# Routed tiles halved in row layout, shared blocks stored plainly and routed results added by scatter, in a kernel with a scan layer and a mixture of experts

## Chip, cores and metric

One NeuronCore of a Trainium2 chip runs one program. The metric is the device time of one execution in microseconds. Six queues of instructions run side by side: TensorE (PE, its weight loads PEld), VectorE (DVE), ScalarE (ACT), GpSimd (POOL), SyncE (SP, here it only issues DMAs). Each works in program order; semaphores order them against each other.

## Reference

The input is 16 sequences of 512 tokens with 128 features. Two layers, each with a normalisation before it and a residual after it:

```python
x = x + state_space(layernorm(x))       # h_t = a*h_(t-1) + B x_t ;  y = C h + D x
x = x + moe(layernorm(x))

# moe, x of 8192 tokens:
shared = (silu(x @ wg.T) * (x @ wu.T)) @ wd.T          # every token
top_id, score = argmax(logits), sigmoid(max(logits))   # logits = x @ gate_w.T, 8 experts
for e in range(8):                                     # the token's one expert
    xe = where(top_id == e, x * score, 0)
    routed += (silu(xe @ wg[e].T) * (xe @ wu[e].T)) @ wd[e].T
return shared + routed
```

The hidden width is 256. So every output row is x1 (the row after the first layer) + shared + routed.

## The kernel before

**First part.** The sequences run in 8 pairs: normalise, transpose, B product, scan along the 512 tokens, C product, residual into `x1`, second normalisation into `n2`, transposed copies `n2T_hi` and `n2T_lo` (fp16, a number as the sum of two halves; `w_split` holds the weights of gate and up likewise, so that a product is three fp16 products). The array `rows` holds for each token x1, n2, its number and its top logit in 264 numbers (1,056 bytes). In groups of 16 token tiles (a tile is 128 tokens) `route` picks the expert of each token and `places` gives it a row in `table`, a DRAM array in which the tokens of an expert lie together. `scatter_row` (L1043) has GpSimd write the 128 whole rows of a token tile to these places by one indirect DMA, 64 in all.

**Shared blocks.** A block is 512 tokens, 16 in all. `shared_gate_up` makes 12 products, ScalarE the silu (`shared_silu`), VectorE the product (`shared_hidden`), `shared_down` 16 fp32 products. The order of blocks is written out: blocks 8 to 15 first (EARLY), then 0 to 7 (LATE). For the first eight VectorE adds the result to x1 in `rows` (`base`, L867), and the rows of these tokens are scattered after that, with x1 + shared in them. The rows of tokens of blocks 0 to 7 are scattered before with x1 alone, and ScalarE copies their shared result over x1 in SBUF (`late_base`, L589). Five of the late blocks (MIDDLE) run before the routed tiles, three behind them. Between the blocks stand parts of other work, by fixed block numbers (`if b == 5:` and so on): the last route, the fp16 halves of routed weights, and the map (`map_counts` to `map_rows`) that says which rows of the table and which expert each routed tile has. SP waits for the map's last step (MAP), the pads that fill up the table, and all scattered rows, then loads the tiles (L277).

**Routed tiles.** There are 39: 32 of 256 rows and 7 of 128, in a ring of 12 buffers. For each: ScalarE computes two tiles' scores from the top logits (`tile_score`) and scales n2 by the score in place (`tile_scale`); TensorE transposes it in fp32 into a PSUM bank (`transpose_tile`); ScalarE copies to fp16 (`tile_hi`), VectorE makes the low half from bank and copy (`tile_lo`); then `routed_gate_up` (12 products), `routed_silu`, `routed_hidden`, `routed_down` (8), and `routed_result`, which adds the tile's x1 part and writes it into the ring buffer. GpSimd scatters 128 rows of 512 bytes to `out` per instruction (`scatter_result`, L1082), two for a whole tile, 71 in all. When all have landed, it adds the eight late blocks of shared results to `out` by accumulating DMAs (`add_late`, L1090).

The order in each queue in the routed stage, for tile j:

```python
PE:  routed_gate_up(j)  routed_down(j - 1)  transpose_tile(j + 2)
ACT: routed_silu(j)  [tile_score(j + 4), j even]  tile_hi(j + 2)  tile_scale(j + 4)
DVE: routed_hidden(j)  routed_result(j - 1)  tile_lo(j + 2)
```

Of the kernel before, what the change touches and what calls it, by code (L numbers as in the profile page):

```python
# [17 lines left out]
ROW = 264  # L18
PITCH = 66
# [9 lines left out]
LATE = 8  # L29
MIDDLE = 5  # L30
# [22 lines left out]
def block_kernel(nc, x, weights, consts, tri_ones, token_ids, pads, out):  # L53
# [12 lines left out]
    EARLY = BLOCKS - LATE  # L66
    FIRST = EARLY + MIDDLE
# [16 lines left out]

    table = nc.dram_tensor("table", (E * REGION + E * SLOTS, ROW), F32, kind="Internal").ap()

    with ExitStack() as ctx:
# [3 lines left out]
        def sem(name):  # L91
# [81 lines left out]
        x_rings = (w_line[:, 0:IN_WEIGHTS * SH * ROW].rearrange("p (k s r) -> p k s r", k=IN_WEIGHTS, s=SH),  # L173
                   sb("x_ring", [P, XRING - IN_WEIGHTS, SH, ROW])[:])
        x_in = [x_rings[k // IN_WEIGHTS][:, k % IN_WEIGHTS] for k in range(XRING)]
        xT_hi = [sb(f"xT_hi{k}", [P, SLOTS], F16) for k in range(XTRING)]
        xT_lo = [sb(f"xT_lo{k}", [P, SLOTS], F16) for k in range(XTRING)]
# [51 lines left out]
        s_first_rows = [sem(f"late_rows_scattered{k}") for k in range(4)]  # L229
# [3 lines left out]
        s_late = sem("sh_late_ready")  # L233
        s_out = sem("output_stored")
        s_xin = [sem(f"tile_loaded{k}") for k in range(XRING)]
        s_xt, s_xh, s_xl = sem("tile_transposed"), sem("tile_hi"), sem("tile_lo")
# [5 lines left out]

        def block_of(b):
            return (b + LATE) % BLOCKS

# [6 lines left out]
        def _(sp):  # L252
# [41 lines left out]
            for k in range(4):  # L294
                sp.wait_ge(s_first_rows[k], 16 * LATE * BT // 4)
                sp.wait_ge(s_scattered[k], 16 * EARLY * BT // 4)
            for j in range(TILES):
                load_tile(j)
            sp.wait_ge(s_out, 16 * LATE)

        @block.tensor
        def _(pe):
# [79 lines left out]
            def shared_gate_up(b):  # L382
                tok = slice(block_of(b) * SEQ, (block_of(b) + 1) * SEQ)
                pe.wait_ge(s_lo, block_of(b) + 1)
# [46 lines left out]
            def routed_gate_up(j):  # L431
# [4 lines left out]
                for kind, banks, used, done in ((0, gate_bank, r_silu, r_g), (1, up_bank, r_hid, r_u)):  # L436
                    after(pe, used, j - 1)
                    for c in range(FC):
                        o = banks[j % 2][:, w * c:w * (c + 1)]
                        mm(o, w_of(kind, e, 0, c), xT_hi[k][:, 0:w], start=True, stop=False)  # L440
                        mm(o, w_of(kind, e, 0, c), xT_lo[k][:, 0:w], start=False, stop=False)  # L441
                        last = mm(o, w_of(kind, e, 1, c), xT_hi[k][:, 0:w], start=False, stop=True)  # L442
# [36 lines left out]
            for b in range(FIRST):  # L479
# [49 lines left out]

        @block.scalar  # L530
        def _(act):
# [57 lines left out]
            def late_base(b):  # L589
                n = block_of(b)  # L590
                act.wait_ge(s_o, b + 1)
                if b == EARLY:
                    for k in range(4):
                        act.wait_ge(s_first_rows[k], 16 * LATE * BT // 4)
                run(x1[:, n * BT:(n + 1) * BT, :], down_bank[b % 2][:].rearrange("p (t d) -> p t d", t=BT),
                    ACT.Copy).then_inc(s_late, 1)
# [31 lines left out]
            def tile_score(j):  # L628
# [7 lines left out]
                run(tanh[:, of, 0:n], tops[:, :, 0:n, 2 * D + 1], ACT.Tanh, scale=l_scale[:, 0:1]).then_inc(s_tanh, 1)  # L636
# [3 lines left out]
            def tile_scale(j):  # L640
                k = j % XRING
                act.wait_ge(s_score, j // 2 + 1)
                for s in range(halves(j)):
                    last = run(x_in[k][:, s, D:2 * D], x_in[k][:, s, D:2 * D], ACT.Copy, scale=score[:, k, s:s + 1])
                last.then_inc(s_scaled, 1)

            def tile_hi(j):
# [3 lines left out]
                run(xT_hi[j % XTRING][:, 0:w], tile_bank[j % 2][:, 0:w], ACT.Copy).then_inc(s_xh, 1)  # L651
# [507 lines left out]
```

## Time and profile before

| | |
|---|---|
| Time, median of 3 runs | 280.43 us (279.65 to 280.5) |
| Profiled execution | 279.88 us, span of its instructions 277.6 us |
| Mean granted TensorE clock | 0.957 |
| Busy: PE, DVE, ACT, POOL | 84%, 65%, 62%, 53% of the span |
| Moved by DMA | 37.83 MB, mean 136 GB/s |

The span runs from the first to the last instruction; the execution takes 2.3 us more. The first part lasts to about 95 us, the shared blocks to about 150 us, the routed tiles to about 255 us, then the late blocks are added. In the rows below, times are microseconds from the start of the span. "idle before" is the time in which the engine stood still ahead of the instructions, and the arrow names what ended it. A row of a timeline with x2 or x8 merges instructions that followed each other. Where a line of the kernel gives way to a number as L87 or L1152, that is a helper or the runtime's own barrier.

### The profile page before, as it was taken

Reading aid. Unit: us, or ns where it says so; the run is one execution under the profiler, and the core shown is the slowest. Engines: PE = TensorE matmul, PEld = TensorE weight load, DVE = VectorE, ACT = ScalarE, POOL = GpSimd, SP = SyncE. Lnnn points to the kernel's source line nnn. Section 1 sums busy time; section 2 is a strip of 40 time slices with the busy share of each in tenths; the row PEclk is TensorE's granted clock in tenths of the full one; section 3 lists DMA queues with packets and bytes.
Section 4 is the critical chain, followed back from the end, with each engine's and each line's share of the span. In section 5 each row is a group of like instructions: output and inputs, shape, how many; then the busy total and the mean of one; then the engine's idle time right before and its main releaser. Section 6 shows DMA issues by size and latency. Waiting matters only on the chain. (4 is left out here: it accounts for less than half of the span.)

```text
span 277.6 us, 6124 instructions
## 1 busy us (share of the span) xinstructions
PE 233.6 (84%) x1891; PEld 181.1 (65%) x1891; DVE 179.9 (65%) x512; ACT 173.0 (62%) x415; POOL 146.2 (53%) x150
## 2 busy tenths in 40 slices
PE   0584988878779999999997699999999999999900
PEld 0263655565367466676774599999999999765700
DVE  3599998799887986559873156666666666644200
ACT  2753988996997984643342686777767676723400
POOL 1000000017777777778770027777777777775940
PEclk9999597999999999999999799999999999999975
DMA  6999500002323223232853923655465543211991
GB/s 210 396 333 327 218 0 0 2 1 101 116 100 119 100 106 110 100 117 97 284 206 105 297 99 93 167 170 172 132 176 165 143 121 96 72 47 50 107 175 22
DMA packets 24862, 37.83 MB, mean 136 GB/s; under 512 B 3680, under 2 KB 16864, under 8 KB 24272
## 3 DMA queue, kind: packets, MB, share of 16 engines
q1 hardware_dynamic: 15264, 22.03, 26.0%
q0 software_dynamic: 9568, 15.41, 19.9%
q8 instruction: 17, 0.28, 0.5%
q14 instruction: 13, 0.11, 0.1%
HBM read 22.03 MB, written 19.73 MB: 150 GB/s over the span
## 5 line engine op out<-in xcount | busy, mean ns | idle before, releaser
L1045 POOL DMA_INDIRECT table<-rows,place x64 | 65.6, 1024 | 60.2 <-DVE place L808 41.1
L1086 POOL DMA_INDIRECT out<-w_full x51 | 49.5, 970 | 33.5 <-DVE w_full L1022 19.5
L1015 DVE SCALAR_TENSOR_TENSOR hid<-bank,h_scale,n1T 128x512 f32<-128x512 f32 (+1 forms) x39 | 27.4, 703 | 29.8 <-ACT n1T L657 28.4
L440 PE MATMUL bank<-xT_hi,w_split 128*128 128x256 f16 (+1 forms) x156 | 40.9, 264 | 0.8 <-DVE xT_lo L1007 0.5
L442 PE MATMUL bank<-xT_hi,w_split 128*128 128x256 f16 (+1 forms) x156 | 40.9, 264 | 0.0
L441 PE MATMUL bank<-xT_lo,w_split 128*128 128x256 f16 (+1 forms) x156 | 40.7, 263 | 0.0
L452 PE MATMUL bank<-w_full,hid 128*128 x284 | 38.7, 277 | 0.1
L587 ACT ACTIVATE n1T<-bank,g_scale 128x512 f32<-128x512 f32 x32 | 21.8, 687 | 23.3 <-PE bank L394 23.1
L452 PEld LDWEIGHTS bank<-w_full,hid 128*128 128x128 f32 x284 | 34.8, 192 | 1.4 <-issue 0.2
L406 PEld LDWEIGHTS bank<-w_full,hid 128*128 128x128 f32 x256 | 32.4, 200 | 1.8
L406 PE MATMUL bank<-w_full,hid 128*128 128x128 f32 x256 | 32.6, 283 | 0.0
L563 ACT ACTIVATE rows<-rows,nb,r 128x128 f32<-128x128 f32 x64 | 25.6, 481 | 6.9 <-DVE nb L764 6.9
L651 ACT ACTIVATE xT_hi<-bank 128x256 f16<-128x256 f32 (+1 forms) x39 | 14.2, 364 | 24.3 <-PE bank L413 24.3
L864 DVE SCALAR_TENSOR_TENSOR hid<-bank,h_scale,n1T 128x512 f32<-128x512 f32 x32 | 23.3, 748 | 9.3 <-ACT n1T L587 8.6
L657 ACT ACTIVATE n1T<-bank,g_scale 128x512 f32<-128x512 f32 (+1 forms) x39 | 25.0, 640 | 2.6 <-PE bank L442 2.4
L549 ACT ACTIVATE n<-rows,nb,r 128x128 f32<-128x128 f32 x64 | 25.4, 480 | 1.0 <-DVE nb L727 1.0
L310 PE MATMUL bank<-const,n 128*128 128x128 f32 x64 | 12.2, 328 | 15.3 <-ACT n L549 15.3
L392 PE MATMUL bank<-n2T_hi,w_split 128*128 128x512 f16 x64 | 24.3, 380 | 0.8 <-DVE w_full L1022 0.4
L394 PE MATMUL bank<-n2T_hi,w_split 128*128 128x512 f16 x64 | 24.3, 379 | 0.0
L393 PE MATMUL bank<-n2T_lo,w_split 128*128 128x512 f16 x64 | 24.2, 379 | 0.0
L1007 DVE TENSOR_TENSOR xT_lo<-bank,xT_hi 128x256 f16<-128x256 f32 (+1 forms) x39 | 15.6, 401 | 13.2 <-PE bank L406 8.9
L1086 POOL DMA_INDIRECT out<-x_ring x20 | 19.4, 970 | 6.1 <-issue 5.5
(142 smaller groups left out, 432.6 us busy)
## 6 DMA issues: line engine op xcount, KB each, us to landing
w_full<-table SPq DMA_DIRECT2D x24, 264.0 KB, 3.0
rows<-in_x SPq DMA_DIRECT2D x8, 512.0 KB, 7.8
w_full<-in_weights SPq DMA_DIRECT2D x3, 1152.0 KB, 12.7
table<-in_pads SPq DMA_DIRECT2D x1, 2112.0 KB, 10.5
table<-in_pads SPq DMA_DIRECT2D x8, 264.0 KB, 4.2
x_ring<-table SPq DMA_DIRECT2D x8, 264.0 KB, 3.3
out<-rows POOLq DMA_DIRECT2D x8, 256.0 KB, 7.8
table<-rows,place POOLq DMA_INDIRECT x64, 2.4
```

The source lines that it names most:

```text
L392: mm(o, w_split[:, 0, kind, 0, f], n2T_hi[:, tok], start=True, stop=False)
L406: last = mm(o, hid[2 * par + c][:, tok], w_full[:, 2, f], start=(c == 0), stop=(c == FC - 1))
L440: mm(o, w_of(kind, e, 0, c), xT_hi[k][:, 0:w], start=True, stop=False)
L441: mm(o, w_of(kind, e, 0, c), xT_lo[k][:, 0:w], start=False, stop=False)
L442: last = mm(o, w_of(kind, e, 1, c), xT_hi[k][:, 0:w], start=False, stop=True)
L452: last = mm(o, hid[j % 4][:, slot], down_of(j, c), start=(c == 0), stop=(c == FC - 1))
L549: last = run(n1[:, t, :], x1[:, q * PT + t, :], ACT.Identity, bias=nb1[q % 2][:, t:t + 1], scale=r1[q % 2][:, t:t + 1])
L563: last = run(n2[:, i, :], x1[:, i, :], ACT.Identity, bias=nb2[q % 2][:, t:t + 1], scale=r2[q % 2][:, t:t + 1])
L657: run(silu[j % 2][:, 0:w], gate_bank[j % 2][:, 0:w], ACT.Silu, scale=g_scale[:, 0:1]).then_inc(r_silu, 1)
L1015: v.scalar_tensor_tensor(out=hid[j % 4][:, 0:w], in0=up_bank[j % 2][:, 0:w], scalar=h_scale[:, 0:1], in1=silu[j % 2][:, 0:w], op0=ALU.mult ...
L1045: g.indirect_dma_start(table[:, :], bass.IndirectOffsetOnAxis(ap=place[:, i:i + 1], axis=0), rows[:, i, :], None).then_inc(done, 16)
L1086: g.indirect_dma_start(out[:, :], bass.IndirectOffsetOnAxis(ap=x_in[k][:, s, 2 * D:2 * D + 1].bitcast(I32), axis=0), x_in[k][:, s, 0:D], N ...
```

## The change

- `table` keeps only n2, number and top logit: 136 numbers a row, 544 bytes. `rows` stays as it is; the scatter takes its last 136 numbers.
- The blocks run in the order 0 to 15, all before the routed tiles. VectorE adds each result to x1 (`base`), and SP stores the block to `out` with a plain DMA (`store_block`), in fixed places of its order: blocks 0 to 8 ahead of the pads, 9 to 11 behind them, 12 to 15 behind the loads of the first four tiles. The rows are scattered without a wait for `base`.
- A tile is split before it is transposed: ScalarE writes the scaled high half in fp16 (`tile_scale`), VectorE the low half from the loaded tile, the score and the high half (`tile_low`), TensorE turns both by products with an fp16 identity, and ScalarE copies both at once from PSUM (`tile_copy`).
- `routed_result` is a copy. The scatter to `out` adds (`compute_op=ALU.add`), and GpSimd waits for all 16 stores before the first one. `late_base` and `add_late` are gone.

```diff
+TILE_ROW = 136
-LATE = 8
-MIDDLE = 5
...
-    table = nc.dram_tensor("table", (E * REGION + E * SLOTS, ROW), F32, kind="Internal").ap()
+    table = nc.dram_tensor("table", (E * REGION + E * SLOTS, TILE_ROW), F32, kind="Internal").ap()
...
+        identity_h = sb("identity_h", [P, P], F16)
+        x_half = [sb(f"x_half{k}", [P, 2, SH, P], F16) for k in range(XTRING)]
+        xT = [sb(f"xT{k}", [P, 2, SLOTS], F16) for k in range(XTRING)]
...
+            def store_block(b):
+                sp.wait_ge(s_base, b + 1)
+                sp.dma_start(out_tiles[:, b * BT:(b + 1) * BT, :], x1[:, b * BT:(b + 1) * BT, :]).then_inc(s_out, 16)
+
+            for b in range(9):
+                store_block(b)
             sp.wait_ge(s_map, 1)
             for e in range(E):
                 store_pads(e)
+            for b in range(9, 12):
+                store_block(b)
...
             for k in range(4):
-                sp.wait_ge(s_first_rows[k], 16 * LATE * BT // 4)
-                sp.wait_ge(s_scattered[k], 16 * EARLY * BT // 4)
-            for j in range(TILES):
+                sp.wait_ge(s_scattered[k], 16 * NT // 4)
+            for j in range(4):
                 load_tile(j)
-            sp.wait_ge(s_out, 16 * LATE)
+            for b in range(12, BLOCKS):
+                store_block(b)
+            for j in range(4, TILES):
+                load_tile(j)
+            sp.wait_ge(s_out, 16 * BLOCKS)
...
-                after(pe, s_base, min(b - 1, EARLY))
-                after(pe, s_late, b - 1 - EARLY)
+                after(pe, s_base, b - 1)
...
-                pe.wait_ge(s_scaled, j + 1)
+                pe.wait_ge(s_xlow, j + 1)
                 after(pe, s_xl, j - 1)
-                for s in range(halves(j)):
-                    last = nc.tensor.transpose(tile_bank[j % 2][:, P * s:P * (s + 1)], x_in[j % XRING][:, s, D:2 * D], identity)
+                w = width(j)
+                for part in range(2):
+                    for s in range(halves(j)):
+                        last = mm(tile_bank[j % 2][:, w * part + P * s:w * part + P * (s + 1)],
+                                  x_half[j % XTRING][:, part, s, :], identity_h[:], start=True, stop=True)
                 last.then_inc(s_xt, 1)
...
                 pe.wait_ge(r_hid, j + 1)
+                if j < 2:
+                    pe.wait_ge(s_base, BLOCKS - 1 + j)
...
+            pe.wait_ge(s_identity, 1)
             load_expert(0)
             transpose_tile(0)
-            shared_down(FIRST - 1)
             transpose_tile(1)
-            pe.wait_ge(s_silu, FIRST * FC)
-            pe.wait_ge(s_hid, FIRST * FC)
+            shared_down(BLOCKS - 1)
+            pe.wait_ge(s_silu, BLOCKS * FC)
+            pe.wait_ge(s_hid, BLOCKS * FC)
             for j in range(TILES):
                 routed_gate_up(j)
-                if j == 0:
-                    pe.wait_ge(s_late, MIDDLE)
                 if j >= 1:
                     routed_down(j - 1)
                 if j + 2 < TILES:
...
                 if j + 1 < TILES:
                     load_expert(j + 1)
 
-            for b in range(FIRST, BLOCKS):
-                if b == FIRST:
-                    pe.wait_ge(r_silu, TILES)
-                    pe.wait_ge(r_hid, TILES)
-                shared_gate_up(b)
-                if b == FIRST:
-                    routed_down(TILES - 1)
-                    pe.wait_ge(r_out, TILES)
-                if b > FIRST:
-                    shared_down(b - 1)
-            shared_down(BLOCKS - 1)
...
+            act.wait_ge(s_const, 16)
+            run(identity_h[:], identity, ACT.Copy).then_inc(s_identity, 1)
...
             def tile_scale(j):
                 k = j % XRING
                 act.wait_ge(s_score, j // 2 + 1)
+                after(act, s_xt, j - XTRING + 1)
                 for s in range(halves(j)):
-                    last = run(x_in[k][:, s, D:2 * D], x_in[k][:, s, D:2 * D], ACT.Copy, scale=score[:, k, s:s + 1])
+                    last = run(x_half[j % XTRING][:, 0, s, :], x_in[k][:, s, 0:D], ACT.Copy, scale=score[:, k, s:s + 1])
                 last.then_inc(s_scaled, 1)
 
-            def tile_hi(j):
+            def tile_copy(j):
                 act.wait_ge(s_xt, j + 1)
                 after(act, r_u, j - XTRING + 1)
                 w = width(j)
-                run(xT_hi[j % XTRING][:, 0:w], tile_bank[j % 2][:, 0:w], ACT.Copy).then_inc(s_xh, 1)
+                run(xT[j % XTRING][:, :, 0:w], tile_bank[j % 2][:, 0:2 * w].rearrange("p (h w) -> p h w", h=2),
+                    ACT.Copy).then_inc(s_xl, 1)
...
+                if b == BLOCKS - 2:
+                    tile_score(0)
+                    tile_scale(0)
+                    tile_scale(1)
+
+            tile_copy(0)
+            tile_copy(1)
             tile_score(2)
             tile_scale(2)
-            tile_hi(1)
             tile_scale(3)
-            late_base(FIRST - 1)
-            act.wait_ge(s_hid, FIRST * FC)
+            act.wait_ge(s_hid, BLOCKS * FC)
             for j in range(TILES):
                 routed_silu(j)
                 if j % 2 == 0 and j + 4 < TILES:
                     tile_score(j + 4)
                 if j + 2 < TILES:
-                    tile_hi(j + 2)
+                    tile_copy(j + 2)
                 if j + 4 < TILES:
                     tile_scale(j + 4)
-
-            act.wait_ge(r_hid, TILES)
-            for b in range(FIRST, BLOCKS + 1):
-                if b < BLOCKS:
-                    shared_silu(b * FC, 0)
-                    shared_silu(b * FC + 1, 1)
-                if b > FIRST:
-                    late_base(b - 1)
...
+            def tile_low(j):
+                k = j % XRING
+                dve.wait_ge(s_scaled, j + 1)
+                for s in range(halves(j)):
+                    last = v.scalar_tensor_tensor(out=x_half[j % XTRING][:, 1, s, :], in0=x_in[k][:, s, 0:D],
+                                                  scalar=score[:, k, s:s + 1], in1=x_half[j % XTRING][:, 0, s, :],
+                                                  op0=ALU.mult, op1=ALU.subtract)
+                last.then_inc(s_xlow, 1)
+
+            for b in range(1, BLOCKS):
+                shared_hidden(b * FC, 0, b)
+                shared_hidden(b * FC + 1, 1, b)
+                base(b - 1)
+                if b == BLOCKS - 1:
+                    tile_low(0)
+                    tile_low(1)
...
-                own = x_in[j % XRING][:, 0:n, 0:D]
                 dve.wait_ge(r_o, j + 1)
-                v.tensor_tensor(out=own, in0=down_bank[j % 2][:, 0:P * n].rearrange("p (s d) -> p s d", s=n), in1=own,
-                                op=ALU.add).then_inc(r_out, 1)
-
-            dve.wait_ge(s_o, FIRST)
-            tile_lo(0)
-            tile_lo(1)
+                v.tensor_copy(x_in[j % XRING][:, 0:n, 0:D],
+                              down_bank[j % 2][:, 0:P * n].rearrange("p (s d) -> p s d", s=n)).then_inc(r_out, 1)
+
+            tile_low(2)
+            base(BLOCKS - 1)
+            tile_low(3)
             for j in range(TILES):
                 routed_hidden(j)
                 if j >= 1:
                     routed_result(j - 1)
-                if j + 2 < TILES:
-                    tile_lo(j + 2)
+                if j + 4 < TILES:
+                    tile_low(j + 4)
...
-                                     rows[:, i, :], None).then_inc(done, 16)
+                                     rows[:, i, D:ROW], None).then_inc(done, 16)
...
+            for i in range(NT):
                 keep_step(i)
-                scatter_row(i, s_first_rows[i % 4])
-            for b in range(EARLY):
-                pool.wait_ge(s_base, b + 1)
-                for t in range(BT):
-                    if t == 2 and b + 2 < FIRST:
-                        pool.wait_ge(s_u, (b + 3) * FC)
-                    scatter_row(block_of(b) * BT + t, s_scattered[t])
+                b = i // BT - BLOCKS // 2
+                if b >= 0 and i % BT == 2:
+                    pool.wait_ge(s_u, (b + 3) * FC)
+                scatter_row(i, s_scattered[i % 4])
...
-                                         bass.IndirectOffsetOnAxis(ap=x_in[k][:, s, 2 * D:2 * D + 1].bitcast(I32), axis=0),
-                                         x_in[k][:, s, 0:D], None).then_inc(s_stored[k], 16)
-
-            def add_late(b):
-                n = block_of(b)
-                pool.wait_ge(s_late, b - EARLY + 1)
-                g.dma_start(out_tiles[:, n * BT:(n + 1) * BT, :], x1[:, n * BT:(n + 1) * BT, :],
-                            accum_op=ALU.add).then_inc(s_out, 16)
-
+                                         bass.IndirectOffsetOnAxis(ap=x_in[k][:, s, D:D + 1].bitcast(I32), axis=0),
+                                         x_in[k][:, s, 0:D], None, compute_op=ALU.add).then_inc(s_stored[k], 16)
+
+            pool.wait_ge(s_out, 16 * BLOCKS)
             for j in range(TILES):
                 scatter_result(j)
             for k in range(XRING):
                 pool.wait_ge(s_stored[k], stored(k, TILES))
-            for b in range(EARLY, BLOCKS):
-                add_late(b)
-            pool.wait_ge(s_out, 16 * LATE)
```

## Rows read from the trace of the kernel before

**Rows 1.** Chain of waits: start, us, what

```profile
253.64 0.97 DMA out<-w_full
...
256.56 10.55 POOL out L1093 x8
```

**Rows 2.** Waits of SP's queue: us in total, times, longest

```profile
SPq L87 <- DMA out<-rows: 37.9, 1, 37.9
SPq L87 <- PEq L87: 4.5, 1, 4.5
```

**Rows 3.** Lines L1086 and L1093: duration ns min/median/max, starts; landing

```profile
L1086 POOL DMA_INDIRECT out<-w_full x51: 967/971/976, 164.4 to 253.6; - x51
L1086 POOL DMA_INDIRECT out<-x_ring x20: 967/971/972, 184.8 to 249.8; - x20
...
DMA to landing us min/median/max: 2.2/2.5/4.8
...
L1093 POOL DMA_DIRECT2D out<-rows x8: 1383/2720/3858, 256.6 to 264.4; - x8
...
DMA to landing us min/median/max: 4.4/7.8/9.3
```

**Rows 4.** Timeline, 144 to 166 and 248.5: start, us, instructions

```profile
144.38 1.95 PE L406 MATMUL bank<-w_full,hid 128*128 128x128 f32 x16
...
148.76 1.95 PE L406 MATMUL bank<-w_full,hid 128*128 128x128 f32 x16
...
149.46 6.57 SPq L279 DMA_DIRECT2D w_full<-table  x8
...
159.41 0.28 PE L440 MATMUL bank<-xT_hi,w_split 128*128 128x256 f16 x1 [0.50 <-DVE xT_lo L1007]
...
163.42 0.27 PE L440 MATMUL bank<-xT_hi,w_split 128*128 128x256 f16 x1
...
163.74 0.41 DVE L1022 TENSOR_TENSOR w_full<-bank,w_full 128x256 f32<-128x256 f32 x1
...
164.43 0.97 POOL L1086 DMA_INDIRECT out<-w_full  x1 [18.32 <-DVE w_full L1022]
...
165.84 0.27 PE L440 MATMUL bank<-xT_hi,w_split 128*128 128x256 f16 x1
...
248.53 0.71 PE L452 MATMUL bank<-w_full,hid 128*128 x4
```

**Rows 5.** Groups by line and form, whole span: busy us, mean ns

```profile
L644 ACT ACTIVATE w_full<-w_full,score 128x128 f32<-128x128 f32 x51 | 17.5, 391 | 0.1
L657 ACT ACTIVATE n1T<-bank,g_scale 128x512 f32<-128x512 f32 x32 | 21.7, 677 | 0.1
...
L570 ACT ACTIVATE n2T_hi<-bank 128x512 f16<-128x512 f32 x16 | 9.3, 589 | 2.7 <-PE bank L342 2.7
...
L871 DVE TENSOR_TENSOR rows<-bank,rows 128x512 f32<-128x512 f32 x8 | 5.5, 690 | 7.0 <-PE bank L406 6.9
...
L850 DVE SCALAR_TENSOR_TENSOR w_split<-w_full,w_mul,w_split 128x256 f16<-128x256 f32 x2 | 0.9, 470 | 0.0
```

**Rows 6.** DMA issues by line: count, KB each, median us to landing

```profile
w_full<-table SPq DMA_DIRECT2D x3, 132.0 KB, 2.2
```

**Rows 7.** Timelines of VectorE and GpSimd where they meet

```profile
87.89 0.86 DVE L850 SCALAR_TENSOR_TENSOR w_split<-w_full,w_mul,w_split 128x256 f16<-128x256 f32 x2
88.27 0.97 POOL L1045 DMA_INDIRECT table<-rows,place  x1 [0.30 <-issue]
...
125.08 2.34 DVE L855 SCALAR_TENSOR_TENSOR w_split<-w_full,w_mul,w_split 128x2048 f16<-128x2048 f32 x1
125.40 2.86 POOL L1045 DMA_INDIRECT table<-rows,place  x1 [0.30 <-issue]
...
141.02 0.42 DVE L958 TENSOR_TENSOR ended<-end_whole,const 128x256 f32<-128x256 f32 x1
141.17 1.10 POOL L1045 DMA_INDIRECT table<-rows,place  x1 [0.30 <-issue]
```

More of the change, by code:

```diff
@@ L228, in block_kernel @@
         s_scattered = [sem(f"rows_scattered{k}") for k in range(4)]
-        s_first_rows = [sem(f"late_rows_scattered{k}") for k in range(4)]
         s_count, s_map = sem("expert_counts_ready"), sem("tile_map_steps")
@@ L382, in shared_gate_up @@
             def shared_gate_up(b):
-                tok = slice(block_of(b) * SEQ, (block_of(b) + 1) * SEQ)
-                pe.wait_ge(s_lo, block_of(b) + 1)
+                tok = slice(b * SEQ, (b + 1) * SEQ)
+                pe.wait_ge(s_lo, b + 1)
                 for c in range(FC):
@@ L439, in routed_gate_up @@
                         o = banks[j % 2][:, w * c:w * (c + 1)]
-                        mm(o, w_of(kind, e, 0, c), xT_hi[k][:, 0:w], start=True, stop=False)
-                        mm(o, w_of(kind, e, 0, c), xT_lo[k][:, 0:w], start=False, stop=False)
-                        last = mm(o, w_of(kind, e, 1, c), xT_hi[k][:, 0:w], start=False, stop=True)
+                        mm(o, w_of(kind, e, 0, c), xT[k][:, 0, 0:w], start=True, stop=False)
+                        mm(o, w_of(kind, e, 0, c), xT[k][:, 1, 0:w], start=False, stop=False)
+                        last = mm(o, w_of(kind, e, 1, c), xT[k][:, 0, 0:w], start=False, stop=True)
                     last.then_inc(done, 1)
@@ L478, in _ @@
             pe.wait_ge(s_h, PAIRS)
-            for b in range(FIRST):
+            for b in range(BLOCKS):
                 shared_gate_up(b)
@@ L635, in tile_score @@
                     act.wait_ge(s_xin[i % XRING], 16 * (i // XRING + 1))
-                run(tanh[:, of, 0:n], tops[:, :, 0:n, 2 * D + 1], ACT.Tanh, scale=l_scale[:, 0:1]).then_inc(s_tanh, 1)
+                run(tanh[:, of, 0:n], tops[:, :, 0:n, D + 1], ACT.Tanh, scale=l_scale[:, 0:1]).then_inc(s_tanh, 1)
                 act.wait_ge(s_tanh, j // 2 + 1)
@@ L657, in routed_silu @@
                 run(silu[j % 2][:, 0:w], gate_bank[j % 2][:, 0:w], ACT.Silu, scale=g_scale[:, 0:1]).then_inc(r_silu, 1)
-            for b in range(1, FIRST):
+            for b in range(1, BLOCKS):
                 shared_silu(b * FC, 0)
@@ L976, in map_rows @@
                 assert map_steps[0] == MAP
-            for b in range(1, FIRST + 1):
-                if b < FIRST:
-                    shared_hidden(b * FC, 0, b)
-                    shared_hidden(b * FC + 1, 1, b)
-                if 1 <= b <= EARLY:
-                    base(b - 1)
+            def tile_low(j):
[6 more added lines that the diff above has]
+                last.then_inc(s_xlow, 1)
+            for b in range(1, BLOCKS):
+                shared_hidden(b * FC, 0, b)
[4 more added lines that the diff above has]
+                    tile_low(1)
                 if b == 1:
@@ L1001, in _ @@
                     map_rows()
-            def tile_lo(j):
-                dve.wait_ge(s_xh, j + 1)
-                after(dve, r_u, j - XTRING + 1)
-                w = width(j)
-                v.tensor_tensor(out=xT_lo[j % XTRING][:, 0:w], in0=tile_bank[j % 2][:, 0:w], in1=xT_hi[j % XTRING][:, 0:w],
-                                op=ALU.subtract).then_inc(s_xl, 1)
             def routed_hidden(j):
@@ L1031, in _ @@
                     routed_result(j - 1)
-                if j + 2 < TILES:
-                    tile_lo(j + 2)
+                if j + 4 < TILES:
+                    tile_low(j + 4)
             routed_result(TILES - 1)
-            for b in range(FIRST, BLOCKS):
-                shared_hidden(b * FC, 0, b)
-                shared_hidden(b * FC + 1, 1, b)
         @block.gpsimd
@@ L1070, in keep_step @@
                     pool.wait_ge(s_bu, min(q + 3, PAIRS))
-            for i in range(LATE * BT):
+            for i in range(NT):
                 keep_step(i)
-                scatter_row(i, s_first_rows[i % 4])
-            for b in range(EARLY):
-                pool.wait_ge(s_base, b + 1)
-                for t in range(BT):
-                    if t == 2 and b + 2 < FIRST:
-                        pool.wait_ge(s_u, (b + 3) * FC)
-                    scatter_row(block_of(b) * BT + t, s_scattered[t])
+                b = i // BT - BLOCKS // 2
+                if b >= 0 and i % BT == 2:
+                    pool.wait_ge(s_u, (b + 3) * FC)
+                scatter_row(i, s_scattered[i % 4])
             def scatter_result(j):
```

38 lines of the change are left out of this document (9 added, 29 removed).

## The prediction

> **What bounds the kernel now.** I read the chain of waits first. It ends in the eight accumulating stores that GpSimd issues from 256.56 us on, and before them stands the last routed scatter, at 253.64 [rows 1]. The waits of SP's own queue give the rest: its wait for those stores ends 4.5 us before the end of the span, at 273.1, and the 4.5 us after it are the closing barrier [rows 2]. So the last 24 us are: the last scatter lands (2.9 us), the stored late blocks are added (16.5 us), barrier (4.5 us).
>
> What sets 253.64? The groups of GpSimd's lines show 71 scatters of 0.97 us, 51 from one half of the ring and 20 from the other, the first at 164.43 [rows 3, 4]. 253.64 less 164.43 is 89.2 us for 70 steps, 1.274 us each. That is 2.55 us for a whole tile, while TensorE starts tiles 2.42 us apart (163.42 is the third, 165.84 the fourth) [rows 4]. The routed stage is GpSimd's issue of scatters, and it begins when the first result is ready. The timeline around it shows why that is at 164.43: shared blocks take 4.38 us each (144.38 to 148.76), TensorE runs out of shared work after the down product of 148.76, the tile loads are issued at 149.46, and the first routed product runs at 159.41 [rows 4]. From there it is 5.0 us to the first scatter.
>
> So two numbers decide: when the first scatter is issued, and what comes behind the last one.
>
> **What the change removes.** The eight adding stores behind the routed results, 16.5 us [rows 1, 2]. Three shared blocks leave the end of TensorE's program (they lay beside the scatters and the stores, so they were worth nothing there). The table row falls from 1,056 to 544 bytes; GpSimd's issue is 0.97 us for a 512-byte row and 0.97 us for a 1,056-byte one [rows 3, 7], so only landing gets shorter, and nothing waits for it. The waits of the row scatters for the shared result go, at no gain: they ran at 1.27 us each.
>
> **What it moves ahead of the routed stage.** TensorE now does blocks 13 to 15 first. Down products start at 148.76 + 4.38 per block: the one of block 14 starts at 161.9 and ends at 163.85 (1.95 us) [rows 4]. SP stores blocks 0 to 11 before the first tile load, so its wait goes from 149.46 to the result of block 11 (148.76 + 1.95 + 0.69 = 151.4), then a store issue; the first four loads go out from 152.4 to 155.1, 0.9 us apart as the eight of the run at 149.46 do. They land by 157.5 and ScalarE wants them at 157.7. This is covered. The twelve earlier stores cost SP some 0.5 us each in a queue that otherwise waits.
>
> Then the hand-over, step by step.
> - VectorE: result of block 14 (0.69) from 163.9 to 164.5, then the low halves of tiles 0 and 1. Each is two operations of 128x128 with both inputs in SBUF. Nearest rows: 0.47 us at 256 elements, 2.34 us at 2,048, hence 1.04 ns an element and 0.34 us at 128 [rows 5, 7]. As consecutive ones overlap a little I take 0.6 a tile: 165.15 and 165.75.
> - TensorE: idle 1.3 us, transposes, down of block 15 from 166.0 to 167.95, routed product 0 at 167.8. That is 8.4 us later than 159.41.
> - ScalarE: one copy per tile of 128x512 to fp16, 0.59 [rows 5], after the transposes: 165.5 to 166.8; score of tiles 2 and 3, two short operations that I put at 0.6 together (an estimate), to 167.4; their four scalings at 0.39, overlapping (0.68 a tile), 168.1 and 168.7; silu of tile 0 to 169.4.
> - VectorE: low half of tile 2 to 168.7, then the result of block 15 to 169.35, low half of tile 3 to 169.95, hidden of tile 0 to 170.7.
> - SP: **the place that I think costs most.** Loads of tiles 4 onward stand behind the store of block 15, which waits for 169.35. Store issue to 169.85, load 4 at 170.3, load 5 at 171.2, landing 2.2 us later for a tile of this size [rows 6]: 173.4.
> - ScalarE has the score of tiles 4 and 5 right behind silu 0, and waits there. Scores to 174.15, copy of tile 2 to 174.75, scaling of tile 4 to 175.4, silu of tile 1 to 176.05. VectorE: hidden of tile 1 to 176.8, and only then the copy of result 0 (0.41), to 177.2. The first scatter follows its result by 0.28, as 164.43 follows 163.74 + 0.41: **177.5**, that is 13.1 us later.
> - GpSimd's own wait for the sixteen plain stores ends earlier: 169.4 + 3 to 4 us is 173.
>
> TensorE sits idle from 171.9 to 174.7 and reaches tile 3 at about 178.0, 12.2 us after 165.84. Its last product group of the routed stage, at 248.53 before, would be near 260.7, with the last result at about 262.6. GpSimd reaches that tile four us later. So in the stage GpSimd still binds, with 4 us in hand for ScalarE, whose work per tile goes from 0.38 to 0.59 us for the copy. Four fp16 transposes in place of two fp32 ones: one pass each over the same columns; between a saving of 0.1 and a loss of 0.2 us a tile (6 us over 32 tiles, of which 4 are covered); I take zero.
>
> **The end, added up.** 177.5 + 89.2 = 266.7 for the last scatter, if a scatter with addition is issued as fast as one without. Behind it 2.9 us as at 253.64 to 256.56, then 4.5 us of barrier [rows 1, 2]. Two costs are unknown.
> - Landing of an adding scatter: the plain one takes 2.5 us, an adding store of four times the size at least 4.4 [rows 3]. So 0 to 1.9 more, once. I take 0.7, nearer to the scatter as the size is its own.
> - VectorE's low halves against GpSimd. At 125.08 an operation with both inputs in SBUF runs 2.34 us, and the scatter that starts inside it takes 2.86 instead of 0.97: it ends 0.84 us behind the operation [rows 7]. So a scatter needs something 0.13 us after its start that a running operation of this kind holds. The short one at 141.02 costs the scatter of 141.17 only 0.13 us, and the pair at 87.89 costs the scatter of 88.27 nothing although the second of the two runs in it [rows 7]. By that, an operation of 0.34 us costs something only if it started less than 0.21 us before the scatter: 2 x 0.21 / 2.42 = 17% of scatters, 0.10 us each, 71 scatters: 1.2 us. Bounds: zero, and the whole remaining pair, 0.6 / 2.42 = 25% by 0.31 us by 71 = 5.5 us. I take 1.3.
>
> The bandwidth of additions is no bound: eight stores of 256 KB in 16.5 us are 127 GB/s [rows 1 to 3]; the scatters need 64 KB in 1.27 us, 51 GB/s.
>
> Sum: 266.7 + 1.3 + 2.9 + 0.7 + 4.5 = 276.1 us of span against 277.6. The profiled execution took 279.88 with that span, 2.3 more, so 278.4; it lies 0.55 below the median of the runs, 280.43, hence between 278.4 and 278.9. I say **278.6**.
>
> The page "SBUF — State Buffer" of the Trainium skill, section "Who interferes with whom", speaks against the change: a VectorE instruction with two SBUF inputs contends with GpSimd's reads and the later one waits for the whole instruction. The long row agrees; the row at 88.27 shows a scatter that loses nothing.
>
> **The rivals.**
> 1. *A scatter with addition costs GpSimd more to issue.* Place: each of the 71. No row shows one. Below: 0.97 us. Above: the shortest adding store, 1.38 us for 512 rows [rows 3], so up to 0.41 each, 29 us. It decides from 0.03 us a scatter on (1.8 us eat the gain). Priced at 0.1: 7.1 us, span 283.2, **285.5**, slower. For it: an addition must read its target too, and issue work may grow. Against: the adding stores needed only 1.4 us for four times the rows. Chance 0.20.
> 2. *The low halves hold GpSimd for their whole pair*, the upper bound above: 4.2 us more, **282.7**, slower. This is the page's rule taken in full, each scatter that meets the pair waiting it out. For it: the long rows; against: the one at 88.27. Chance 0.12.
> 3. *ScalarE or TensorE sets the routed pace.* Silu 0.68, copy 0.59, scalings 0.68 and every other tile 0.67 for scores (the same estimate with its hand-over) make 2.29 us on average, 2.62 in a tile with scores [rows 5]. If each tile took 2.62, 32 tiles would end 6.4 us later than at 2.42, of which 4 are in hand: 2.4 us, **280.9**, no change or slightly slower. Chance 0.12.
> 4. *The stall at the start is not there or is short*, because loads or stores get through faster than I think, or the result of tile 0 isn't held by them: first scatter at 172.5 to 173, bound by the store of block 15. Then about **274**, faster. Chance 0.13.
>
> Forecast 0.43, with a range of its own from 276.5 to 280.5.
>
> **How the numbers follow.** 0.3% is 0.84 us, about what a measurement tells from no change: faster is below 279.6, slower above 281.3. The forecast is four fifths on the fast side, one fifth within (0.35 and 0.08); rival 4 is faster (0.13); rival 3 splits into 0.02 faster, 0.06 same, 0.04 slower; rivals 1 and 2 are slower (0.32, less 0.02 for mild forms). Faster 0.50, same 0.16, slower 0.34. The range for 8 in 10 goes from 274 (rival 4) to 287 (rival 1 up to 0.12 us a scatter).
>
> **What would show each step.** In the changed kernel's profile: no adding stores in the chain; first scatter to `out` near 177.5, with ScalarE's tanh of tiles 4 and 5 waiting some 3 to 4 us for a load; TensorE's first routed product near 167.8; scatters 0.97 us, a few of them stretched by up to 0.3; last one near 268, and 8 us from there to the end. The forecast is wrong if the median scatter is not 0.97, if GpSimd waits for VectorE's results in mid stage, or if shared blocks 13 to 15 take more than 4.4 us each because VectorE has their results to add as well.

## The result, and the profile after

| | before | after |
|---|---|---|
| Time, median | 280.47 us (4 runs) | 318.12 us (317.9 to 319.39, 4 runs) |
| Ratio of after to before | | 1.136 (95% interval 1.132 to 1.140) |
| Profiled execution; span of its instructions | 279.88 us; 277.6 us | 317.9 us; 316.1 us |
| First routed scatter starts | 164.43 us | 177.60 us |
| Last routed scatter starts | 253.64 us | 307.90 us |
| From there to the end of the span | 24.0 us | 8.2 us |
| Mean granted TensorE clock | 0.957 | 0.923 |

The change makes the kernel 13.6% slower; the prediction was 278.6 us with a range from 274 to 287. The span grows by 38.5 us, and the table splits that: first scatter +13.2, the 70 steps to the last one 130.3 instead of 89.2 (+41.1), and the end behind it −15.8. Two of the runs below were taken at a time when the kernel before itself took 332.79 us instead of some 280, and they are compared with that figure.

The chain of waits of the changed kernel (start, us, what) shows no store after the scatters, as the change says; what it ends in is the last scatter. It goes back two scatters only [rows 1 for the kernel before]:

```profile
305.74 0.30 issue
306.04 1.55 POOL out L1064
...
307.90 1.55 POOL out L1064
```

The scatters' line in the changed kernel: duration in ns (min/median/max), first and last start; what ended GpSimd's idle time before them (us, times); and the landing. The kernel before is in [rows 3]:

```profile
L1064 POOL DMA_INDIRECT out<-w_full x51: 1552/1552/1667, 177.6 to 307.9; - x51
L1064 POOL DMA_INDIRECT out<-x_ring x20: 1552/1552/1555, 207.6 to 302.3; - x20
...
  DVE w_full L1006: 31.8, 1
  issue: 20.4, 67
  DVE x_ring L1006: 0.3, 1
  DMA out<-w_full: 0.3, 1
  DMA out<-x_ring: 0.3, 1
...
DMA to landing us min/median/max: 3.2/3.3/4.9
```

The median is 1.552 us where it was 0.971, and the minimum is the median: every single scatter has the price, not some that met something. To see that nothing else is the pace, read the idle times: one wait of 31.8 us for the first result, and 0.30 us before each of the other 70, whatever ended it. So GpSimd never waits for a result in the stage, and the price is paid at each of the 70 steps. The timeline of GpSimd shows the first of them (start, us, and what ended the idle time before it):

```profile
177.60 1.62 POOL L1064 DMA_INDIRECT out<-w_full  x1 [31.81 <-DVE w_full L1006]
179.52 1.57 POOL L1064 DMA_INDIRECT out<-w_full  x1 [0.30 <-issue]
181.40 1.56 POOL L1064 DMA_INDIRECT out<-w_full  x1 [0.30 <-issue]
183.26 1.55 POOL L1064 DMA_INDIRECT out<-w_full  x1 [0.30 <-issue]
```

The hand-over, from the timeline of the changed kernel [rows 4]. It is what ScalarE, VectorE and SP do between the shared and the routed stage:

```profile
164.30 1.13 DVE L964 SCALAR_TENSOR_TENSOR x_half<-w_full,score,x_half 128x128 f16<-128x128 f32 x4
...
165.72 2.00 PE L410 MATMUL bank<-w_full,hid 128*128 128x128 f32 x16
...
167.56 0.27 PE L447 MATMUL bank<-xT,w_split 128*128 128x256 f16 x1
...
169.91 3.04 SPq L273 DMA_DIRECT2D w_full<-table  x4
...
173.36 0.30 ACT L627 ACTIVATE tanh<-w_full,l_scale 128x4 f32<-128x4 f32 x1 [4.20 <-DMA w_full<-table]
...
174.71 0.28 PE L447 MATMUL bank<-xT,w_split 128*128 128x256 f16 x1 [2.98 <-ACT xT L643]
...
175.45 0.42 PE L447 MATMUL bank<-xT,w_split 128*128 128x256 f16 x1
...
176.40 0.42 DVE L1006 COPY w_full<-bank 128x256 f32<-128x256 f32 x1
```

ScalarE waits 4.20 us for tiles 4 and 5, TensorE 2.98 us behind it, and the first result is copied at 176.40. (175.45 shows one more cost, which doesn't reach the first result: behind that gap TensorE's products take 0.42 us instead of 0.27. The granted clock is 0.50 from 175.3 to 178.7 us, the lower of its two levels, and 1.00 ahead of the gap and from 178.8 us on; the product that the first result needs had run at 170.41.)

### The profile page after: what moved, and what is told of

Same layout as the page of the kernel before. It is cut to its first block and busy times, and to the rows that moved or that the text cites. A ratio compares the mean times of both kernels' runs of the same rounds, so it can differ in the third digit from the quotient of the medians.

```text
span 316.1 us, 6296 instructions
## 1 busy us (share of the span) xinstructions
PE 241.8 (76%) x1962; PEld 185.0 (59%) x1962; DVE 190.3 (60%) x552; ACT 174.6 (55%) x408; POOL 177.3 (56%) x142
## 5 line engine op out<-in xcount | busy, mean ns | idle before, releaser
L1064 POOL DMA_INDIRECT out<-w_full x51 | 79.4, 1558 | 47.1 <-DVE w_full L1006 31.8
L1026 POOL DMA_INDIRECT table<-rows,place x64 | 65.6, 1025 | 60.0 <-DVE place L790 41.1
L447 PE MATMUL bank<-xT,w_split 128*128 128x256 f16 (+1 forms) x156 | 42.5, 273 | 18.7 <-ACT xT L643 18.7
L461 PE MATMUL bank<-w_full,hid 128*128 x284 | 43.2, 297 | 3.9 <-DVE hid L1000 3.7
L449 PE MATMUL bank<-xT,w_split 128*128 128x256 f16 (+1 forms) x156 | 42.4, 273 | 0.0
L461 PEld LDWEIGHTS bank<-w_full,hid 128*128 128x128 f32 x284 | 37.8, 206 | 7.8 <-issue 7.1
L448 PE MATMUL bank<-xT,w_split 128*128 128x256 f16 (+1 forms) x156 | 42.3, 272 | 0.0
L964 DVE SCALAR_TENSOR_TENSOR x_half<-w_full,score,x_half 128x128 f16<-128x128 f32 x51 | 15.7, 349 | 39.0 <-ACT x_half L636 39.0
L1064 POOL DMA_INDIRECT out<-x_ring x20 | 31.0, 1552 | 6.1 <-issue 5.8
L410 PEld LDWEIGHTS bank<-w_full,hid 128*128 128x128 f32 x256 | 31.0, 192 | 2.0
L410 PE MATMUL bank<-w_full,hid 128*128 128x128 f32 x256 | 31.3, 275 | 0.0
L447 PEld LDWEIGHTS bank<-xT,w_split 128*128 x156 | 15.8, 101 | 23.0 <-issue 21.0
L643 ACT ACTIVATE xT<-bank 128x512 f16<-128x512 f32 (+1 forms) x39 | 21.4, 550 | 9.9 <-PE bank L419 9.9
```

The source lines that it names most:

```text
L410: last = mm(o, hid[2 * par + c][:, tok], w_full[:, 2, f], start=(c == 0), stop=(c == FC - 1))
L447: mm(o, w_of(kind, e, 0, c), xT[k][:, 0, 0:w], start=True, stop=False)
L448: mm(o, w_of(kind, e, 0, c), xT[k][:, 1, 0:w], start=False, stop=False)
L449: last = mm(o, w_of(kind, e, 1, c), xT[k][:, 0, 0:w], start=False, stop=True)
L461: last = mm(o, hid[j % 4][:, slot], down_of(j, c), start=(c == 0), stop=(c == FC - 1))
L1026: g.indirect_dma_start(table[:, :], bass.IndirectOffsetOnAxis(ap=place[:, i:i + 1], axis=0), rows[:, i, D:ROW], None).then_inc(done, 16)
```

## The experiments

**The addition off the routed scatters, all else as changed (the routed results overwrite the shared ones).**

```diff
-                                         x_in[k][:, s, 0:D], None, compute_op=ALU.add)
+                                         x_in[k][:, s, 0:D], None)
```

> The changed kernel with the addition taken off its 71 routed scatters and nothing else (the routed results overwrite the shared ones, so the sum is left out). Theory A, the addition itself makes each scatter dearer for GpSimd to issue (1.55 us against 0.97): scatters go back to 0.97 us, first one still near 177.6, last one near 266.8, span 275 to 276, time about 277.5. Rival B, the scatters are slow because VectorE's new low halves with two SBUF inputs hold GpSimd up: the scatters stay at 1.5 us and the time near 318. Rival C, part of the 0.58 us is each: something between, 1.2 us a scatter and a time near 295.

277.14 us (276.74 to 277.99), 0.991 of the kernel before (0.988 to 0.994), span 275.6. Two rows of its timeline of GpSimd, the first scatter and the last one:

```profile
177.98 0.96 POOL L1064 DMA_INDIRECT out<-w_full  x1 [33.19 <-DVE w_full L1006]
...
266.68 0.96 POOL L1064 DMA_INDIRECT out<-w_full  x1 [0.30 <-issue]
```

Rivals B and C fall: with VectorE's low halves still there, scatters take 0.96 us. The addition alone is worth 41 us, and all the rest of the change, taken together, is 2.6 us faster than the kernel before, which took 279.79 us beside it. 70 steps in 88.7 us are 1.267 each.

**The addition put into the kernel before (it adds to memory that holds nothing yet).**

```diff
-                                         x_in[k][:, s, 0:D], None).then_inc(s_stored[k], 16)
+                                         x_in[k][:, s, 0:D], None, compute_op=ALU.add).then_inc(s_stored[k], 16)
```

> The kernel before with an addition on its 71 routed scatters and nothing else (they add to memory that nothing was stored to, so the output values mean nothing). Theory A: every scatter 1.55 us, 1.86 from one to the next, first one still at 164.4, last one at 294.5, then 3.7 us to land, the eight adding stores 16.5, barrier 4.5: span 319, time 321. Rival B: nothing in this kernel has VectorE's low halves with two SBUF inputs, so scatters stay at 0.97 and the time at 280.

321.62 us in two runs, 1.149 of the kernel before (1.146 to 1.153), span 319.8, against 321 and 319 expected. GpSimd's line by form (busy us, mean ns):

```profile
L1086 POOL DMA_INDIRECT out<-w_full x51 | 79.4, 1556 | 34.4 <-DVE w_full L1022 19.4 <-issue 14.6 <-DVE x_ring L1022 0.3
```

The same price from the other side, in a kernel without anything else of the change.

**What the price hangs on.** The form of the scatter goes round from tile to tile.

```diff
-                                         x_in[k][:, s, 0:D], None, compute_op=ALU.add).then_inc(s_stored[k], 16)
+            FORMS = ((P, D, True), (P, D // 2, True), (P // 2, D, True), (P, D, False), (P // 2, D, False), (P // 4, D, True))
...
+                rows_of, cols, op = FORMS[j % len(FORMS)]
```

> The changed kernel with the form of the routed scatter changed from tile to tile, in turn: 128 rows of 512 bytes with addition; 128 rows of 256 bytes with addition (into another array); 64 rows of 512 bytes with addition; 128 rows of 512 bytes without; 64 rows without; 32 rows with addition (rows, columns and sums are left out, so the output values mean nothing). If the price of the addition goes by the row (descriptors written), 256-byte rows cost 1.55 as well, 64 rows with addition about 1.55 less half of what 128 rows cost above a fixed part, and the addition costs 0.29 us at 64 rows. If it goes by bytes, 256-byte rows take about 1.26. If it is a fixed price per instruction, 64 rows with addition stand 0.58 above 64 rows without.

Timeline of GpSimd, one round, two instructions of each form (the 256-byte ones go to `narrow`; L1075 is the form without addition):

```profile
181.39 1.56 POOL L1072 DMA_INDIRECT narrow<-w_full  x1 [0.30 <-issue]
183.25 1.55 POOL L1072 DMA_INDIRECT narrow<-w_full  x1 [0.30 <-issue]
185.11 1.42 POOL L1072 DMA_INDIRECT out<-w_full  x1 [0.31 <-issue]
186.84 1.42 POOL L1072 DMA_INDIRECT out<-w_full  x1 [0.30 <-issue]
188.56 0.99 POOL L1075 DMA_INDIRECT out<-w_full  x1 [0.30 <-issue]
189.86 0.98 POOL L1075 DMA_INDIRECT out<-w_full  x1 [0.30 <-issue]
191.14 0.90 POOL L1075 DMA_INDIRECT out<-w_full  x1 [0.30 <-issue]
192.34 0.89 POOL L1075 DMA_INDIRECT out<-w_full  x1 [0.30 <-issue]
193.54 1.40 POOL L1072 DMA_INDIRECT out<-w_full  x1 [0.30 <-issue]
195.24 1.35 POOL L1072 DMA_INDIRECT out<-w_full  x1 [0.30 <-issue]
```

Bytes don't matter (256-byte rows 1.55). Half the rows save 0.14 us with addition and 0.09 without. At 64 rows the addition costs 1.42 − 0.90 = 0.52, at 128 rows 0.57: most of it is a fixed price per instruction. (At 32 rows no plain scatter was run beside the 1.40 and 1.35.) What GpSimd does in it no profile shows. The time, 302.69 us in one run, compares nothing, as the forms are mixed.

**Ten tile loads ahead of the last block stores.**

```diff
-            for j in range(4):
+            for j in range(10):
                 load_tile(j)
             for b in range(12, BLOCKS):
                 store_block(b)
-            for j in range(4, TILES):
+            for j in range(10, TILES):
```

> The changed kernel with ten instead of four tile loads ahead of the stores of blocks 12 to 15 in SP's queue, all else as it is. My step on the start says that the loads of tiles 4 and 5, behind the store of block 15, make ScalarE wait 4.2 us and hold the first result: without that the first scatter comes 4 to 5 us earlier, near 173, bound by the landing of block 15's store, and the time is 313 to 314.5 against 318. Rival: GpSimd's wait for all sixteen stores is what holds the first scatter: it stays at 177 or comes later, and the time stays at 318.

313.84 us (313.35 to 314.29), 4.3 less than the changed kernel; first scatter:

```profile
172.94 1.62 POOL L1064 DMA_INDIRECT out<-w_full  x1 [28.79 <-DVE w_full L1006]
```

The first scatter comes 4.7 us earlier, but 0.3 of that stands ahead of the hand-over, where the two kernels are the same: the down product of block 15 starts at 165.38 here and at 165.72 in the changed kernel. Counted from it, the first scatter follows after 7.56 us instead of 11.88. So the SP order costs 4.3 us, and the rival (the wait for the stores) falls.

**Both edits: plain scatters and loads first.**

> The changed kernel with both edits at once: no addition on the routed scatters (the sum is left out) and ten tile loads ahead of the last four block stores. If the two costs are separate and simply add, the first scatter is at 172.9 to 173.3, scatters are 0.96 us and the time is 277.1 less 4.3 to 4.7: 272.4 to 272.8. Rival: with plain scatters, ScalarE and VectorE, which have longer work per tile now, become the pace of the stage once the scatters start earlier; then GpSimd waits for results and half or more of the 4.5 us is lost: 274.5 or more.

331.44 us beside 332.79 for the kernel before, ratio 0.997 (0.993 to 1.001). In this trace GpSimd waits for results 21 times (70.4 us in all, 34.5 of them before the first scatter), so its scatters are not the pace and the run doesn't answer the question. The same kernel again, beside 279.35 us for the kernel before:

> The same kernel as e5_plain_loads (no addition on the routed scatters, so the sum is left out; ten tile loads ahead of the last four block stores), run again, because there the kernel before itself took 333 us against 280 elsewhere. Same expectation: if the two costs simply add, the first scatter is at 172.9 to 173.3 and the time 272.4 to 272.8; if ScalarE and VectorE become the pace of the stage, 274.5 or more.

273.10 us (272.58 to 273.54), 0.978 of the kernel before (0.974 to 0.981): 4.0 less than with plain scatters alone. First scatter:

```profile
173.98 0.96 POOL L1064 DMA_INDIRECT out<-w_full  x1 [28.85 <-DVE w_full L1006]
```

The two costs add. The time is just above the expected 272.4 to 272.8 and far from the rival's 274.5. The missing 0.3 us stands ahead of the hand-over again: the down product of block 15 starts at 166.41 here and at 166.08 in the run with plain scatters alone, and counted from it the first scatter follows after 7.57 us instead of 11.90, the same 4.3 us as with additions. Behind it the 70 steps take 88.9 us against 88.7, and the idle time before each is 0.30 us, so GpSimd doesn't wait for ScalarE or VectorE and the rival has no part.

**A version that keeps plain scatters: six middle blocks.** The kernel before with `MIDDLE = 6`.

> The kernel before with six instead of five late blocks between the early ones and the routed tiles. TensorE stands idle for 4.1 us there (150.7 to 154.8, then works at half clock until 158.5). If that hole takes one more block, the first scatter moves by less than 1 us either way, and as GpSimd's scatters set the pace and the adding stores wait for the last scatter only, the time is the same: 279 to 281. Rival: the extra block pushes the routed stage back by its 4.4 us: 284.

278.03 us (276.96 to 279.53), 0.995 (0.993 to 0.997). That is a gain where I expected none: the first scatter moves by 1.8 us, to 162.64 from 164.43, and the time by as much. TensorE no longer idles for 4.1 us there, and its last down product ahead of the tiles takes 1.95 us instead of 3.43. The granted clock from 154.8 to 158.5 us is 0.54 in the kernel before and 1.00 here. In the kernel before:

```profile
154.84 0.63 PE L413 MATMUL bank<-const,w_full 128*128 128x128 f32 x2 [4.14 <-ACT w_full L644]
155.27 3.43 PE L406 MATMUL bank<-w_full,hid 128*128 128x128 f32 x16
```

With six middle blocks:

```profile
154.96 1.95 PE L406 MATMUL bank<-w_full,hid 128*128 128x128 f32 x16
```

**Another end: load back, add on VectorE, store.** In the kernel before and with six middle blocks:

```diff
+            for n in range(BACK):
+                sp.dma_start(rows[:, n * BT:(n + 1) * BT, D:2 * D], out_tiles[:, n * BT:(n + 1) * BT, :]).then_inc(s_back[n], 16)
+            for n in range(BACK):
+                sp.wait_ge(s_sum, n + 1)
+                sp.dma_start(out_tiles[:, n * BT:(n + 1) * BT, :], x1[:, n * BT:(n + 1) * BT, :]).then_inc(s_out, 16)
...
+                v.tensor_tensor(out=own, in0=rows[:, n * BT:(n + 1) * BT, D:2 * D], in1=own, op=ALU.add).then_inc(s_sum, 1)
```

> The kernel before with another end: when all routed results have landed, SP loads the routed rows of the eight late blocks back into SBUF (plain DMAs), VectorE adds the shared result and SP stores the sum (plain DMAs), in place of the eight adding stores of GpSimd. If the 16.5 us of the adding stores are the price of the addition in the DMA engines (127 GB/s), 4 MB of plain traffic at the 300 to 400 GB/s that the loads of the start show take 10 to 13 us with 5 us of latency beside it: 2 us less to 2 us more than before, 278 to 282, held back here by VectorE, which comes to the sums only after the last hidden product at 262. Rival: memory is the limit, not the addition: 4 MB then takes as long as or longer than 2 MB added, 284 or more.

281.93 us, 1.007 (1.004 to 1.009).

> Both of the two: six late blocks ahead of the routed tiles, and the end by loading back, adding on VectorE and storing. VectorE is free for the sums from 258 on, so the loads at 256.6 + 2.5 us and on are met as they land: last store lands near 270, time 276 to 278. Rival as for the run with the changed end alone: no gain, 280 or more.

281.22 us, 1.005 (1.003 to 1.007). Five blocks that way and three by adding stores:

> As the last one, but only late blocks 0 to 4 go by way of SBUF, and blocks 5 to 7 are added by GpSimd's adding stores at the same time. If the two ways use the DMA engines at 127 GB/s for additions and three times that for plain data, the three blocks cost 6.2 us and the other five 6.5 to 8: 13 to 14 us, no better than 277. If latencies and VectorE bind the plain way, the mixture is 1 to 2 us faster: 275 to 276.

279.75 us, 1.000 (0.998 to 1.001). None of the three gains. The first lies at the upper edge of its range (278 to 282), the second came out as its rival said (280 or more), the third as "no better than 277". With six middle blocks SP's last wait ends at 270.3 us of the span, 0.5 earlier than with adding stores (270.8), and the end took that back. The queue of SP in the kernel with six middle blocks and all eight blocks by this end (us in total, times, longest), where this wait is the closing one [rows 2]:

```profile
SPq L88 <- PEq L88: 9.0, 1, 9.0
```

9.0 us against 4.5, and 6.6 with five blocks that way and three by adding stores. The next two runs ask whose they are. SP alone waits for its stores:

```diff
-            for b in range(EARLY + BACK, BLOCKS):
-                add_late(b)
-            pool.wait_ge(s_out, 16 * LATE)
```

> The kernel with six middle blocks and the end by loading back, adding on VectorE and storing, with GpSimd's own wait for the last stores taken off: SP alone waits for them, GpSimd is done when its scatters have landed. In that kernel 9.0 us pass from SP's last wait to the end of the span, where the kernel before has 4.5. If the 9 us are GpSimd waking and closing after SP's stores, they shrink to 4.5 or less and the time is near 276.5; if they belong to SP's own closing after its stores, nothing changes: 281.

328.34 us beside 332.79 for the kernel before, 0.989 (0.983 to 0.996); within its trace the interval is

```profile
SPq L88 <- PEq L88: 0.2, 1, 0.2
```

so the interval was GpSimd's closing behind its own last wait. What that is worth in time is not shown, as this kernel was not run again where the kernel before takes 280 us. (An estimate: 281.22 less 8.8 is 272.4 us.) The same with the adding stores, on the kernel with six middle blocks:

```diff
                 add_late(b)
-            pool.wait_ge(s_out, 16 * LATE)
```

> The kernel before with six middle blocks and without GpSimd's own wait for the adding stores at its end: SP alone waits for them, as it did before too. With GpSimd's wait, 4.5 us pass from SP's last wait to the end of the span. In the run where SP alone waited for SP's stores that interval was 0.2 us instead of 9.0. If it is GpSimd's closing after a long wait, it goes here too: span 271, time 273 to 274.5. If it belongs to the adding stores, nothing changes: 278.

276.40 us (276.18 to 278.27), 0.991 (0.988 to 0.995): the fastest kernel measured here that computes everything, 42 us below the changed one and 1.6 us below the one with six middle blocks and GpSimd's wait. It is neither what I expected if the interval went (273 to 274.5) nor if it stayed (278). The interval is 3.4 us, not 0.2:

```profile
SPq L87 <- PEq L87: 3.4, 1, 3.4
```

So 1.1 us of the 4.5 went with GpSimd's wait, and the rest stays when its last instructions are adding stores. Why is open.

## Why the prediction was wrong

**The step that failed is one term, the cost of issuing an adding scatter.** The sum took "266.7 for the last scatter, if a scatter with addition is issued as fast as one without". It is not: 1.86 us a step against 1.274, 70 times, 41 us; with the addition alone taken off it is 1.267 again. The rival was on paper, with its place and its sign right, but its upper bound was wrong as well: 0.41 us, from the shortest adding store of 512 rows (1.38 us in all). Measured is 0.58. I had bounded an indirect instruction by a direct one, as if the cost went by rows. The run with six forms shows that it doesn't: most of it is a fixed amount for the instruction. The shortest direct adding store, 1.38 us in all, is below the 1.55 of an adding scatter; what of it is addition no run shows. And I priced it at 0.1, gave it 0.20, and cut the range at 0.12 us a scatter, though I had written down that no row shows an addition on an indirect DMA. As the unknown is paid 71 times, the range had to reach 308 even by my own upper bound (278.6 and 29), and that would still have missed.

**The steps that held.**
- The start: first scatter 177.5 predicted, 177.60 measured. TensorE's first routed product 167.8, measured 167.56; ScalarE's wait for tiles 4 and 5 "3 to 4 us", 4.20; the first result at 176.8 to 177.2, measured 176.40 to 176.82. The run with ten loads ahead confirms the cause. That 177.5 came out to 0.1 is partly luck: the first result was ready 0.4 us earlier than predicted, and the first scatter follows it by 0.78 us, not by the 0.28 of the kernel before. The changed kernel and the four edits of it that ran beside 280 us all show 0.78 to 0.79; why is open.
- Shared blocks kept their 4.38 us: down products start at 148.59, 152.96, 157.34 and 161.71 (block 14, 161.9 predicted), and that of block 15 at 165.72 (166.0 predicted).
- Issue of a scatter doesn't go by its bytes: 0.97 at both sizes before, 1.55 at 256 and 512 bytes with addition.
- fp16 transposes at no price: four take 0.39 us, two fp32 ones took 0.38, and with plain scatters GpSimd stays the pace.
- Landing: 0.7 more predicted for an addition, measured 3.3 against 2.5 at the median [rows 3], and against 2.2 in the changed kernel without addition.
- The end: 8.1 us predicted (2.9 + 0.7 + 4.5), 8.2 measured. But with plain scatters it is 8.9, from 266.68 to 275.6, with a shorter landing. So the agreement is partly luck: the closing is no constant (0.2 to 9.0 us in these runs where SP's queue shows it), and I had taken it for one.
- VectorE's low halves against GpSimd: 1.3 us predicted, less found. In the run with plain scatters four are visibly stretched, by 0.04 to 0.12 us, 0.3 us in all. One of them, and the operation it met:

```profile
222.16 0.61 DVE L964 SCALAR_TENSOR_TENSOR x_half<-x_ring,score,x_half 128x128 f16<-128x128 f32 x2 [0.71 <-ACT x_half L636]
```

```profile
222.27 1.08 POOL L1064 DMA_INDIRECT out<-w_full  x1 [0.30 <-issue]
```

The scatter starts 0.11 us after the first low half and takes 0.12 more than 0.96: the first one (0.35 us) ends at 222.51, the scatter asks for its input at about 222.40. The second low half of the pair, which runs until 222.77, doesn't hold it. That fits the reading of [rows 7]. The Trainium skill (page "SBUF — State Buffer", section "Who interferes with whom") states that a VectorE instruction with two SBUF inputs contends with a GpSimd instruction that reads SBUF. The trace agrees, with 0.12 us for this scatter; the whole remaining pair as a price, my upper bound of 5.5 us, did not come.

With the one term set right, and nothing for the low halves, the sum is 177.5 + 130.3 + 8.1 = 315.9 against a span of 316.1.

## What to carry to other kernels

Where a stage is paced by the issue of one kind of instruction, a new flag on that instruction is the first thing to measure, and as long as no row shows it, the range has to hold its upper bound times the count. Here an addition in an indirect DMA was paid mostly by the instruction and not by the byte, so its price is the count of instructions times 0.58 us. Eight adding stores of 256 KB at the end (16.5 us, for 2 MB) cost this kernel less than the addition on 71 scatters (41 us, for 4.5 MB), since the scatters already set the pace. And where SP and GpSimd wait for the same last transfers, try the version in which SP alone does: it took 1.6 us off where its time can be compared.

## What the runs showed that I had not expected

- An indirect DMA with addition costs GpSimd 1.55 us against 0.97 at 128 rows, 1.42 against 0.90 at 64, and 1.35 to 1.40 at 32, where no plain one was run.
- Between SP's last wait and the end of the span stand 4.5 us in the kernel before, 9.0 when GpSimd waits for SP's stores with its scatters long done, 6.6 when it waits for both kinds of store, 0.2 when it doesn't wait, 3.4 when it has just issued adding stores and doesn't wait.
- 4 MB of plain traffic (2 MB read, 2 MB written) in place of 2 MB of additions took as long. From the first transfer's issue to SP's last wait the two ends take 16.1 us (six middle blocks) and 16.5 (kernel before), which is 262 GB/s against 127; in their busiest stretches of 3 us they move 334 and 180.
